# A windowed ratio with group statistics on one core: half of every second row group of batch 1 takes its denominator from channel sums made on VectorE and one wide matmul

## The chip, the cores and the metric

One of the eight cores of a Trainium2 chip runs the whole program. The metric is the device time of one execution in microseconds (us), as the median of several executions. A profile is one more execution of the same program. Engines are named as the profile names them: PE (TensorE), DVE (VectorE), ACT (ScalarE), POOL (GpSimd) and SP (SyncE, which issues the transfers).

## The reference, cut to what matters

x has the shape 2 x 128 x 128 x 192 (batch, rows, columns w, channels) in float32. It is normalised in 32 groups of 6 channels to v, and then:

```python
s     = box(v, over w, 5)
num   = box(s * s, over channels, 20)
d     = box(box(v * v, over w, 5), over channels, 20)
denum = d * c0 * c1          # c1: how many of the 5 columns lie inside, 5 but at the edges
out   = x + nan_to_num(num / denum, nan=1.0)
```

A box is a sliding sum with zeros beyond the ends. The one over channels takes 10 channels below and 9 above. In the kernel S stands for s, U for the sum of squares over w, D for the denominator (with its sign turned) and N for the numerator.

## The kernel before

Columns w lie on the 128 partitions, and rows and channels lie along each partition. A **pair** is two rows, 384 values a partition; a **duo** is two pairs, 768 values. There are 32 duos a batch and 64 in all, and the main loops of all engines run over the duos n = 0 to 63. Every PSUM tile (S, U, D, N) has two banks, one for each pair of a duo.

Both sums are matmuls with banded matrices. `box5` sums over w: the data are the stationary operand and the band b5 (or b5d, the band times -c1) moves through, so the result is transposed, channels on the partitions. It takes three matmuls of 128 columns a pair, six a duo. `box20` sums over channels: the transposed result is stationary and a band `b20` of 20 ones, already divided by the variance of each channel, moves through, which turns the result back. It takes matmuls of 138, 147 and 137 columns a pair, six a duo. The profile counts each float32 matmul as two instructions, so six matmuls stand as x12.

In batch 1 a duo passes so: POOL subtracts the group mean (`centre`, xc). PE makes S from xc with b5, and ACT squares it into a slot of xs (`square_s`). ACT squares xc (`square_xc`), PE makes U with b5d, and ACT copies U to u (`keep_u`). PE makes D from u and N from the squared S. ACT takes the reciprocal root of D (`take_root`) and squares it (`square_root`) into q. DVE makes t1 = D times q, t2 = N times q, and ratio = (t1 + 2) times t2 (`quotient`, one step of Newton's method). POOL adds the ratio to x (`finish`), and SP stores two duos at a time.

The order on each engine is fixed by the program, and semaphores connect the engines. One turn n of the main loops has

- PE: `sum_d(n)`, `box_u(n + 2)`, `sum_n(n)`, `box_s(n + 2)`. The first waits for t1 of duo n - 1, and the third for the ratio of duo n - 1.
- ACT: `take_root(n)`, `square_root(n)`, `keep_u(n + 2)`, `square_xc(n + 3)`, `square_s(n + 2)`.
- DVE: `quotient(n)`, with the late statistics of batch 1 between its steps at n = 29 (`spread_late`) and n = 30 (`scale_late_bands`).
- POOL: `centre(n + 4)`, `finish(n)`.

In batch 0 the boxes of the raw input of the first 28 duos are made ahead, while x arrives; the statistics of batch 1 are gathered on DVE during batch 0. The mean of batch 1 is known at n = 29, and POOL waits for it (semaphore mean_ready) before it centres duo 32, the first of batch 1.

`link` makes a DVE instruction whose result the next one waits for.

Of the kernel before, what the change touches and what calls it, by code (L numbers as in the profile page):

```python
# [6 lines left out]
ALU = mybir.AluOpType  # L7
# [4 lines left out]
GROUPS = 32  # L12
# [5 lines left out]
EPS = 1e-5  # L18
# [26 lines left out]

HALF = STEPS // 2
XC2_SLOT, S2_SLOT, LATE_SLOTS = HALF, HALF + 2, 2
LOADS = 8
LOAD_STEPS = STEPS // LOADS
LOAD_DUOS = LOAD_STEPS * STEP_DUOS  # L50
# [26 lines left out]
def window_ratio_kernel(nc, x, out):  # L77
    ctx = ExitStack()
    with ctx:
# [41 lines left out]
        offsets_wide_ps = S[:, 1, 0:CHUNKS * 128].rearrange("p (j w) -> p j w", j=CHUNKS)  # L121
        offsets_ps = offsets_wide_ps[:, :, 0:COEFS]

        loaded0 = [sem(f"loaded0_{j}") for j in range(LOADS)]
        loaded1 = [sem(f"loaded1_{j}") for j in range(len(LATE_SETS))]
        bands_ready = sem("bands_ready")
# [14 lines left out]
        mean_ready = sem("mean_ready")  # L141
        b20_ready = sem("b20_ready")
        inv_ready = sem("inv_ready")
        xc_ready = sem("xc_ready")
        xc2_ready = sem("xc2_ready")
        s_ready = sem("s_ready")
# [30 lines left out]
        def slot(n):  # L177

            t = n % DUOS // STEP_DUOS
            if batch(n) == 0:  # L180
                return RAW + t
            return t if t < HALF else RAW + t - HALF

        def x_rows(n, duos=1):

# [80 lines left out]
        @block.gpsimd  # L266
        def _(pool):
            own = [0]

            def band(ap, conditions):  # L270

                nc.gpsimd.memset(ap, 1.0).then_inc(pool_own, 1)
                own[0] += 1
                for base, channel, pattern in conditions:
                    pool.wait_ge(pool_own, own[0])
                    nc.gpsimd.affine_select(out=ap, in_=ap, compare_op=ALU.is_ge, fill=0.0, base=base,
                                            pattern=pattern, channel_multiplier=channel)\
# [36 lines left out]

            def finish(n):

                pool.wait_ge(ratio_ready, n + 1)
                nc.gpsimd.tensor_tensor(x_flat(n), x_flat(n), ratio[:, n % RATIO_RING, :], ALU.add)\  # L318
                  .then_inc(out_ready, 1)

            for j in range(LOADS):
                pool.wait_ge(loaded0[j], 16)
            pool.wait_ge(mean_ready, 1)
            for n in range(CENTRE_AHEAD):
                centre(n)
            for n in range(TOTAL - 1):
                m = n + CENTRE_AHEAD
                if m == DUOS:
                    for j in range(len(LATE_SETS)):
                        wait_loaded1(pool, j)  # L330
                    pool.wait_ge(mean_ready, 2)
                if m < TOTAL:
                    centre(m)
                finish(n)

        @block.scalar
        def _(act):
# [7 lines left out]
            def square_xc(n):  # L345

                act.wait_ge(xc_ready, n + 1)
                if n == RAW_DUOS:
                    act.wait_ge(n_ready, (XC2_SLOT + LATE_SLOTS) * STEP_DUOS)
                if not is_raw(n) and not is_raw(n - LATE_RING):  # L350
                    act.wait_ge(u_ready, n - LATE_RING + 1)
                nc.scalar.activation(xc2_of(n), xc_of(n), ACT.Square).then_inc(xc2_ready, 1)  # L352

            def keep_u(n):

                act.wait_ge(u_ready, n + 1)
                if n >= U_RING:
                    act.wait_ge(d_ready, n - U_RING + 1)
                nc.scalar.activation(pairs(u[:, n % U_RING, :]), in_bank(U), ACT.Copy).then_inc(us_ready, 1)  # L359

            def square_s(n):

# [57 lines left out]
            for n in range(TOTAL):  # L420
                take_root(n)
                square_root(n)
                if n + BOX_AHEAD < TOTAL:
                    keep_u(n + BOX_AHEAD)
                if n + SQUARE_AHEAD < TOTAL:
                    square_xc(n + SQUARE_AHEAD)
                square_box(n + BOX_AHEAD)

        @block.tensor
        def _(pe):  # L430

            def box5(bank, rows, weights):

                for i in range(DUO):
                    for j in range(CHUNKS):
                        chunk, at = slice(128 * j, 128 * (j + 1)), i * PCOLS + 128 * j
                        mm = nc.tensor.matmul(bank[:, i, chunk], rows[:, at:at + 128], weights[:, :],  # L437
                                              start=True, stop=True)
                return mm

            def box20(bank, data, b):

                for i in range(DUO):
# [24 lines left out]
            def box_u(n):  # L468

                pe.wait_ge(xc2_ready, n + 1)  # L470
                if n:
                    pe.wait_ge(us_ready, n)
                box5(U, xc2_of(n), b5d).then_inc(u_ready, 1)

            def sum_d(n):

                pe.wait_ge(us_ready, n + 1)
                if d_prev(n) >= 0:
                    pe.wait_ge(t1_ready, d_prev(n) + 1)
                if n == 1:  # L480
                    pe.wait_ge(edges_ready, 2)
                box20(d_bank(n), u[:, n % U_RING, :], batch(n)).then_inc(d_ready, 1)

            def sum_n(n):

# [22 lines left out]
            def average_squares(b):  # L508
# [3 lines left out]
                for j in range(CHUNKS):  # L512
                    out, cols = (var_ps[1][:, j:j + 1], 1) if b else (var_wide_ps[:, j, :], 128)
                    mm = nc.tensor.matmul(out, flat[:, 128 * j:128 * (j + 1)], averager[0][:, 0:cols],
                                          start=True, stop=True)
                return mm

            def keep_warm():
# [39 lines left out]
        def _(dve):  # L558
# [63 lines left out]
            def scale_late_bands():  # L622

                link(fold_variance(1))
                for j in range(CHUNKS):
                    cols = slice(SPAN_AT[j], SPAN_AT[j + 1])
                    ins = nc.vector.tensor_scalar(b20[:, cols], b20[:, cols], inv_var[:, j:j + 1], None, ALU.mult)
                ins.then_inc(b20_ready, 1)

            def keep_offsets():  # L630
                link(nc.vector.tensor_copy(offsets[:, :, :], offsets_ps))
# [10 lines left out]

            def quotient(n, before_ratio=None):

                dve.wait_ge(q_ready, n + 1)
                if n >= RATIO_RING:
                    dve.wait_ge(out_ready, n - RATIO_RING + 1)
# [48 lines left out]
            for n in range(TOTAL - 1):  # L696
                if n == JOIN_AT:
                    for j, g in unmeasured:
# [5 lines left out]
                quotient(n, before_ratio=spread_late if n == MEAN_AT else scale_late_bands if n == VAR_AT else None)  # L704
# [25 lines left out]
```

## Time and profile before

| what | us |
|---|---|
| median of three executions | 393.49 |
| the three executions | 393.3, 393.49, 395.51 |
| profiled execution, its own time | 395.41 |
| its span, first to last instruction | 393.6 |
| PE busy in the span | 371.3 |
| ACT, DVE, POOL busy in the span | 277.0, 262.5, 233.6 |

The span is counted in the trace from its first instruction, and every start time in the rows below is from there. The ends of matmuls are modelled, so the spacing from the start of one group to the start of the next tells more than a duration. A row `[2.48 <-ACT q L401]` says that the engine stood idle for 2.48 us before this instruction, until line 401 on ACT released it. On ACT, DVE and POOL a row's duration can overlap the start of the next instruction by up to some 0.1 us, so there too the spacing of starts is used.

### The profile page before, as it was taken

The numbers are of one execution on the slowest core, as the hardware profiler recorded it, in microseconds if no ns is written. First come the engines' busy times: TensorE is split into PE (matmuls) and PEld (weight loads), VectorE is DVE, ScalarE is ACT, GpSimd is POOL, SyncE is SP. The second block draws the span as 40 slices with busy tenths as digits, with TensorE's granted clock in tenths as the row PEclk, the third lists the DMA queues.
The fourth block names the chain that finished last, engine by engine and source line by source line (L and its number), as shares of the span: only waits on it lengthen the run. The fifth ranks groups of instructions, "written<-read, shape, count | busy, mean of one in ns | idle before, by whom it ended". The sixth has DMA issues, their size and how long they took to land.

```text
span 393.6 us, 8026 instructions
## 1 busy us (share of the span) xinstructions
PE 371.3 (94%) x3124; PEld 369.7 (94%) x3124; DVE 262.5 (67%) x555; ACT 277.0 (70%) x368; POOL 233.6 (59%) x150
## 2 busy tenths in 40 slices
PE   1999988999999999999889999999999999999982
PEld 1999988999999999999789999999999999999982
DVE  2999952676679999999766455445544455445544
ACT  1455549999999998996447667766777667766751
POOL 4000054887888888886088656765676556765431
PEclk9999989999999999999899999999999999999997
DMA  8999100588988952222203122222211222222213
GB/s 243 327 328 328 57 2 0 162 242 269 292 274 288 296 189 82 81 82 82 80 3 110 50 82 80 82 82 82 80 59 38 66 82 82 80 82 82 80 42 121
DMA packets 66485, 50.84 MB, mean 129 GB/s; under 512 B 912, under 2 KB 66448, under 8 KB 66448
## 3 DMA queue, kind: packets, MB, share of 16 engines
q1 hardware_dynamic: 66448, 50.34, 41.2%
q8 instruction: 25, 0.41, 0.4%
q14 instruction: 12, 0.10, 0.1%
HBM read 25.17 MB, written 25.17 MB: 128 GB/s over the span
## 4 chain that ended last, share of the span: by engine, by line
PE 82%; DVE 6%; issue 4%; ACT 4%; DMA 2%; POOL 0%; DVEq 0%; POOLq 0%; ACTq 0%
PE N L446 20%; PE U L437 19%; PE D L446 16%; PE S L437 16%; PE N L437 5%; PE S L446 4%; DVE late_triples L577 2%; DMA xs<-x 2%; DVE ratio L649 2%; DVE N L652 1%; ACT xs L377 1%; ACT q L395 1%; PE D L500 1%; PE U L521 1%; ACT q L401 1%
## 5 line engine op out<-in xcount | busy, mean ns | idle before, releaser
L318 POOL TENSOR_TENSOR xs<-xs,ratio 128x768 f32<-128x768 f32 x63 | 114.5, 1818 | 91.6 <-DVE ratio L658 91.6
L312 POOL TENSOR_TENSOR xc<-xs,mean_c 128x768 f32<-128x768 f32 x64 | 116.9, 1828 | 60.3 <-DVE mean_c L586 46.2
L649 DVE SCALAR_TENSOR_TENSOR ratio<-D,q 128x768 f32<-128x768 f32 x51 | 48.7, 955 | 91.7 <-ACT q L401 91.7
L652 DVE SCALAR_TENSOR_TENSOR N<-N,q 128x768 f32<-128x768 f32 x64 | 61.6, 963 | 7.5 <-PE N L446 3.9
L658 DVE SCALAR_TENSOR_TENSOR ratio<-ratio,N 128x768 f32<-128x768 f32 x64 | 61.1, 954 | 6.8 <-DVE N L652 0.5
L395 ACT ACTIVATE q<-D 128x768 f32<-128x768 f32 x51 | 41.4, 811 | 30.0 <-PE D L446 30.0
L368 ACT ACTIVATE xs<-S 128x768 f32<-128x768 f32 x36 | 29.2, 811 | 38.7 <-PE S L437 38.7
L401 ACT ACTIVATE q<-q 128x768 f32<-128x768 f32 x64 | 54.0, 844 | 2.0
L437 PE MATMUL U<-b5d,xs 128*128 128x128 f32 x432 | 54.1, 275 | 1.1 <-ACT xs L352 1.1
L437 PE MATMUL S<-b,xc 128*128 128x128 f32 x432 | 54.6, 277 | 0.0
L446 PE MATMUL N<-b_r,xs 128*128 128x138 f32 (+2 forms) x384 | 53.3, 288 | 0.0
L446 PE MATMUL D<-b,u 128*128 128x138 f32 (+2 forms) x384 | 51.6, 283 | 1.4 <-DVE ratio L649 1.4
L437 PEld LDWEIGHTS U<-b5d,xs 128*128 128x128 f32 x432 | 51.2, 191 | 1.3 <-ACT xs L352 1.3
L437 PEld LDWEIGHTS S<-b,xc 128*128 128x128 f32 x432 | 51.9, 194 | 0.0
L446 PE MATMUL N<-b,xs 128*128 128x138 f32 (+2 forms) x384 | 51.6, 283 | 0.2 <-DVE ratio L658 0.2
L359 ACT ACTIVATE u<-U 128x768 f32<-128x768 f32 x64 | 50.9, 795 | 0.3 <-PE U L437 0.2
L446 PEld LDWEIGHTS D<-b,u 128*128 128x128 f32 x384 | 48.5, 190 | 1.6 <-issue 1.6
L446 PEld LDWEIGHTS N<-b_r,xs 128*128 128x128 f32 x384 | 49.4, 193 | 0.0
L446 PEld LDWEIGHTS N<-b,xs 128*128 128x128 f32 x384 | 48.5, 190 | 0.4 <-issue 0.4
L577 DVE BATCH_NORM_STATS2 ratio<-xs 128x6 f32<-128x96 f32 x256 | 40.9, 252 | 6.0 <-DMA xs<-x 6.0
L437 PE MATMUL U<-b5d,xc 128*128 128x128 f32 x336 | 42.6, 277 | 1.2 <-ACT u L359 1.0
L437 PEld LDWEIGHTS U<-b5d,xc 128*128 128x128 f32 x336 | 40.3, 193 | 1.5 <-issue 1.2
(67 smaller groups left out, 382.2 us busy)
## 6 DMA issues: line engine op xcount, KB each, us to landing
out<-xs SPq DMA_DIRECT2D x31, 768.0 KB, 3.8
xs<-x SPq DMA_DIRECT2D x8, 1536.0 KB, 14.7
xs<-x SPq DMA_DIRECT2D x16, 768.0 KB, 5.4
out<-xs SPq DMA_DIRECT2D x2, 384.0 KB, 2.9
```

The source lines that it names most:

```text
L312: nc.gpsimd.tensor_tensor(pairs(xc[:, n % XC_RING, :]), pairs(x_flat(n)), mean, ALU.subtract)\
L318: nc.gpsimd.tensor_tensor(x_flat(n), x_flat(n), ratio[:, n % RATIO_RING, :], ALU.add)\
L359: nc.scalar.activation(pairs(u[:, n % U_RING, :]), in_bank(U), ACT.Copy).then_inc(us_ready, 1)
L368: nc.scalar.activation(pairs(s2_of(n)), in_bank(S), ACT.Square).then_inc(s2_ready, 1)
L395: nc.scalar.activation(pairs(q[:, n % Q_RING, :]), in_bank(d_bank(n)), ACT.Abs_reciprocal_sqrt, bias=-TINY)\
L401: nc.scalar.activation(q[:, n % Q_RING, :], q[:, n % Q_RING, :], ACT.Square).then_inc(q_ready, 1)
L437: mm = nc.tensor.matmul(bank[:, i, chunk], rows[:, at:at + 128], weights[:, :], start=True, stop=True)
L446: mm = nc.tensor.matmul(bank[:, i, first:end], data[:, at:at + 128], b20_r[b][:, SPAN_AT[j]:SPAN_AT[j + 1]], start=j == 0, stop=j == CHUNK ...
L577: return nc.vector.bn_stats(to.rearrange("p g a b -> p (g a b)"), rows)
L649: nc.vector.scalar_tensor_tensor(t1, in_bank(d_bank(n)), -TINY, pairs(q[:, n % Q_RING, :]), ALU.add, ALU.mult).then_inc(t1_ready, 1)
L652: nc.vector.scalar_tensor_tensor(in_bank(N), in_bank(N), TINY, pairs(q[:, n % Q_RING, :]), ALU.add, ALU.mult).then_inc(t2_ready, 1)
L658: nc.vector.scalar_tensor_tensor(t1, t1, 2.0, in_bank(N), ALU.add, ALU.mult).then_inc(ratio_ready, 1)
```

## The change

Fifteen duos of batch 1, n = 35, 37, ... 63 (`summed(n)`), treat their second pair in another way. The first pair of such a duo goes as before, so box_u, keep_u, square_xc and box20 for D work on one pair in place of two. S and N stay as they are.

For the second pair POOL multiplies xc by the reciprocal standard deviation of its channel's group (`scale_c`) into a line in SBUF, `padded`, with 10 zeros between the two rows (`normalise`). ACT squares the line of 424 values into bank 1 of U, which box_u doesn't use in this duo (`square_line`). DVE makes the sums of 20 neighbours from two scans and one addition (`sum_windows`): one scan runs backward and starts anew every 20 values, the other runs forward and starts anew at the same places, and a window of 20 is the sum of one value of each. PE then takes the result as moving operand of one matmul with b5d as stationary operand, 384 columns wide, straight into bank 1 of D.

Once, where the batches meet, the change adds what this needs: three memsets on POOL (`clear_sums`), one more small matmul for the group variance, two small steps on DVE, a reciprocal root on ACT at the end of turn 30, and on DVE in turn 31 four small steps and two copies (`spread_scale`).

```diff
+SUM_SLOT = HALF + 4
+FIRST_SUMMED, SUMMED_EVERY = DUOS + 3, 2
+PITCH = C + C_LO
+REACH = PITCH + C
+BLOCKS = (REACH + C_WIN - 1) // C_WIN
+LINE = BLOCKS * C_WIN
+PADDED = PAIR * PITCH + C_WIN
...
@@ POOL
+            def normalise(n):
+                k = nth_summed(n)
+                if k:
+                    pool.wait_ge(squares_ready, k)
+                else:
+                    pool.wait_ge(scale_ready, 1)
+                pool.wait_ge(xc_ready, n + 1)
+                pair = xc_of(n)[:, PCOLS:2 * PCOLS].rearrange("p (r c) -> p r c", r=PAIR)
+                nc.gpsimd.tensor_tensor(rows_of(padded[:, C_LO:PADDED]), pair,
+                                        scale_c.rearrange("p (r c) -> p r c", r=PAIR), ALU.mult)\
+                  .then_inc(scaled_ready, 1)
+            def clear_sums():
+                pool.wait_ge(n_ready, RAW_DUOS)
+                nc.gpsimd.memset(padded, 0.0).then_inc(pool_own, 1)
+                nc.gpsimd.memset(restart, 1.0).then_inc(pool_own, 1)
+                pool.wait_ge(pool_own, own[0] + 2)
+                nc.gpsimd.memset(restart.rearrange("p (a b) -> p a b", b=C_WIN)[:, :, 0], 0.0).then_inc(bands_ready, 1)
...
                     pool.wait_ge(mean_ready, 2)
+                    clear_sums()
                 if m < TOTAL:
                     centre(m)
+                if summed(m):
+                    normalise(m)
                 finish(n)
@@ ACT
+            def square_line(n):
+                act.wait_ge(scaled_ready, nth_summed(n) + 1)
+                act.wait_ge(us_ready, n)
+                nc.scalar.activation(squares_ps, padded, ACT.Square).then_inc(squares_ready, 1)
...
                     square_xc(n + SQUARE_AHEAD)
+                if summed(n + SQUARE_AHEAD):
+                    square_line(n + SQUARE_AHEAD)
                 square_box(n + BOX_AHEAD)
+                if n == VAR_AT:
+                    act.wait_ge(group_var_ready, 1)
+                    nc.scalar.activation(mean_sum[:, :], dev_sum[:, :], ACT.Abs_reciprocal_sqrt).then_inc(root_ready, 1)
@@ PE, box_u and sum_d
-                box5(U, xc2_of(n), b5d).then_inc(u_ready, 1)
+                if summed(n - 1):
+                    pe.wait_ge(of_20_ready, nth_summed(n - 1) + 1)
+                box5(U, xc2_of(n), b5d, own_pairs(n)).then_inc(u_ready, 1)
...
-                box20(d_bank(n), u[:, n % U_RING, :], batch(n)).then_inc(d_ready, 1)
+                mm = box20(d_bank(n), u[:, n % U_RING, :], batch(n), own_pairs(n))
+                if summed(n):
+                    pe.wait_ge(of_20_ready, nth_summed(n) + 1)
+                    mm = nc.tensor.matmul(D[:, 1, 0:PCOLS], b5d[:, :], of_20, start=True, stop=True)
+                mm.then_inc(d_ready, 1)
@@ DVE
+            def sum_windows(n):
+                k = nth_summed(n)
+                dve.wait_ge(squares_ready, k + 1)
+                if k == 0:
+                    dve.wait_ge(bands_ready, 3)
+                link(nc.vector.tensor_tensor_scan(rising[:, 0:LINE][:, ::-1], restart, squares_ps[:, 0:LINE][:, ::-1], 0.0,
+                                                  ALU.mult, ALU.add))
+                before = squares_ps[:, C_WIN - 1:C_WIN - 1 + REACH]
+                link(nc.vector.tensor_tensor_scan(before, before, restart[:, 0:REACH], 0.0, ALU.add, ALU.mult))
+                if k:
+                    dve.wait_ge(d_ready, n - SUMMED_EVERY + 1)
+                nc.vector.tensor_tensor(of_20.rearrange("p (r c) -> p r c", r=PAIR), rows_of(squares_ps[:, C_WIN - 1:PADDED]),
+                                        rows_of(rising), ALU.add).then_inc(of_20_ready, 1)
...
             def quotient(n, before_ratio=None):
+                if summed(n + 2):
+                    sum_windows(n + 2)
                 dve.wait_ge(q_ready, n + 1)
```

How the order moves on PE, in a turn n of batch 1 whose duo and whose duo n + 2 are summed (n odd). First the turn of before, from sum_d(n) to box_s(n + 2):

```order
L446 MATMUL D<-b,u 128x138
L446 MATMUL D<-b,u 128x147
L446 MATMUL D<-b,u 128x137
L446 MATMUL D<-b,u 128x138
L446 MATMUL D<-b,u 128x147
L446 MATMUL D<-b,u 128x137
L437 MATMUL U<-b5d,xs 128x128 x6
```

and the same stretch now:

```order
L520 MATMUL D<-b,u 128x138
L520 MATMUL D<-b,u 128x147
L520 MATMUL D<-b,u 128x137
L561 MATMUL D<-xs,b5d 128x384
L511 MATMUL U<-b5d,xs 128x128 x3
```

Three matmuls of D give way to a wide one, and three of U are gone; the six of N and the six of S behind them stay. In turns with even n nothing changes on PE.

On DVE the end of `quotient(n)` for even n and the start of the next one, before (t1 is L649, t2 L652, ratio L658):

```order
L649 SCALAR_TENSOR_TENSOR ratio<-D,q 128x768
L652 SCALAR_TENSOR_TENSOR N<-N,q 128x2x384
L658 SCALAR_TENSOR_TENSOR ratio<-ratio,N 128x768
L649 SCALAR_TENSOR_TENSOR ratio<-D,q 128x768
L652 SCALAR_TENSOR_TENSOR N<-N,q 128x2x384
```

and now, where the list prints a scan under the name of SCALAR_TENSOR_TENSOR (L738 and L741 are the scans, L744 the addition):

```order
L768 SCALAR_TENSOR_TENSOR ratio<-D,q 128x768
L771 SCALAR_TENSOR_TENSOR N<-N,q 128x2x384
L777 SCALAR_TENSOR_TENSOR ratio<-ratio,N 128x768
L738 SCALAR_TENSOR_TENSOR xs<-xs,U 128x400
L741 SCALAR_TENSOR_TENSOR U<-U,xs 128x394
L744 TENSOR_TENSOR xs<-U,xs 128x384
L768 SCALAR_TENSOR_TENSOR ratio<-D,q 128x768
```

The three new steps stand between the ratio of an even duo and t1 of the odd one behind it.

On POOL where the batches meet, before, with `centre(32)` as the third row:

```order
L312 TENSOR_TENSOR xc<-xs,mean_c 128x768 [waits s_ready,xc2_ready]
L318 TENSOR_TENSOR xs<-xs,ratio 128x768 [waits ratio_ready]
L312 TENSOR_TENSOR xc<-xs,mean_c 128x768 [waits xc2_ready,mean_ready,s_ready,loaded1_1,loaded1_0]
L318 TENSOR_TENSOR xs<-xs,ratio 128x768 [waits ratio_ready]
L312 TENSOR_TENSOR xc<-xs,mean_c 128x768 [waits s_ready,xc2_ready]
```

and now:

```order
L348 TENSOR_TENSOR xc<-xs,mean_c 128x768 [waits s_ready,xc2_ready]
L354 TENSOR_TENSOR xs<-xs,ratio 128x768 [waits ratio_ready]
L373 MEMSET xs 128x424 [waits mean_ready,n_ready,loaded1_1,loaded1_0]
L374 MEMSET xs 128x400
L376 MEMSET xs 128x20 [waits pool_own]
L348 TENSOR_TENSOR xc<-xs,mean_c 128x768 [waits s_ready,xc2_ready]
L354 TENSOR_TENSOR xs<-xs,ratio 128x768 [waits ratio_ready]
```

The memsets stand behind the wait for the mean and ahead of `centre(32)`.

## Rows read from the trace of the kernel before

**Rows 1.** Windows: us, busy us of PE, PEld, DVE, ACT, POOL, granted clock, DMA share, GB/s.
```profile
230.00:378.00 148.00, 148.00 (x1278) 148.00 (x1277) 76.13 (x80) 103.70 (x133) 93.07 (x52) 1.00 0.22 71
```

**Rows 2.** The chain that ended last, one turn: start us, us, what.
```profile
301.02 1.45 PE D L446 x12
302.47 1.34 PE U L437 x12
303.81 1.45 PE N L446 x12
305.25 1.34 PE S L437 x12
```

**Rows 3.** Timeline, one turn of batch 1: start us, us, engine, instruction.
```profile
300.86 1.61 PE L446 MATMUL D<-b,u 128*128 128x138 f32 x12
...
304.23 0.96 DVE L649 SCALAR_TENSOR_TENSOR ratio<-D,q 128x768 f32<-128x768 f32 x1 [2.48 <-ACT q L401]
305.29 0.97 DVE L652 SCALAR_TENSOR_TENSOR N<-N,q 128x768 f32<-128x768 f32 x1
306.36 0.95 DVE L658 SCALAR_TENSOR_TENSOR ratio<-ratio,N 128x768 f32<-128x768 f32 x1
...
302.51 0.81 ACT L395 ACTIVATE q<-D 128x768 f32<-128x768 f32 x1 [0.57 <-PE D L446]
303.35 0.84 ACT L401 ACTIVATE q<-q 128x768 f32<-128x768 f32 x1
...
301.83 1.81 POOL L318 TENSOR_TENSOR xs<-xs,ratio 128x768 f32<-128x768 f32 x1 [1.98 <-DVE ratio L658]
```

**Rows 4.** Timeline of PE around one matmul of 192 columns, in the load stage.
```profile
21.69 0.49 PE L500 MATMUL D<-ratio,averager 128*128 128x192 f32 x2
22.01 1.50 PE L437 MATMUL S<-b,xs 128*128 128x128 f32 x12
```

**Rows 5.** Timeline where the batches meet: POOL, PE, DVE, ACT.
```profile
198.47 1.82 POOL L312 TENSOR_TENSOR xc<-xs,mean_c 128x768 f32<-128x768 f32 x1 [12.11 <-issue]
...
205.57 1.82 POOL L312 TENSOR_TENSOR xc<-xs,mean_c 128x768 f32<-128x768 f32 x1
...
201.22 1.60 PE L437 MATMUL U<-b5d,xs 128*128 128x128 f32 x12 [1.14 <-ACT xs L352]
202.66 0.73 PE L514 MATMUL N<-averager,ssq_c 128*128 128x1 f32 x6
203.25 1.69 PE L446 MATMUL N<-b_r,xs 128*128 128x138 f32 x12
...
208.90 1.68 PE L446 MATMUL N<-b_r,xs 128*128 128x138 f32 x12
...
205.85 0.15 DVE L619 TENSOR_SCALAR inv_var<-N 128x3 f32<-128x3 f32 x1
...
207.81 0.94 DVE L658 SCALAR_TENSOR_TENSOR ratio<-ratio,N 128x768 f32<-128x768 f32 x1
...
207.76 0.81 ACT L395 ACTIVATE q<-D 128x768 f32<-128x768 f32 x1 [0.58 <-PE D L446]
```

**Rows 6.** Groups by line and form, POOL: mean ns of one behind the comma.
```profile
L272 POOL MEMSET b<- 128x128 f32 x1 | 0.2, 205 | 0.3 <-POOLq L723 0.3
...
L272 POOL MEMSET b<- 128x74 f32 x1 | 0.2, 162 | 0.0
```

**Rows 7.** The same view, DVE.
```profile
L627 DVE TENSOR_SCALAR b<-b,inv_var 128x138 f32<-128x138 f32 x1 | 1.2, 1232 | 0.0
...
L586 DVE COPY mean_c<-N 128x192 f32<-128x192 f32 x2 | 0.6, 347 | 0.0
...
L627 DVE TENSOR_SCALAR b<-b,inv_var 128x147 f32<-128x147 f32 x1 | 0.3, 287 | 0.0
```

**Rows 8.** Timeline of the tail: t1 of duo 62, and sum_d(63) behind it.
```profile
382.19 0.96 DVE L649 SCALAR_TENSOR_TENSOR ratio<-D,q 128x768 f32<-128x768 f32 x1 [2.48 <-ACT q L401]
...
383.29 1.68 PE L446 MATMUL D<-b,u 128*128 128x138 f32 x12 [1.41 <-DVE ratio L649]
```

More of the change, by code:

```diff
@@ L122, in window_ratio_kernel @@
         offsets_ps = offsets_wide_ps[:, :, 0:COEFS]
+        sums = xs[:, SUM_SLOT * STEP:(SUM_SLOT + 2) * STEP, :].rearrange("p r c -> p (r c)")
+        padded, restart = sums[:, 0:PADDED], sums[:, PADDED:PADDED + LINE]
+        rising, of_20 = sums[:, 1024:1024 + PADDED], sums[:, 1536:1536 + PCOLS]
+        scale_c = sums[:, 2048:2048 + PCOLS]
+        rows_of = lambda line: line[:, 0:PAIR * PITCH].rearrange("p (r c) -> p r c", r=PAIR)[:, :, 0:C]
+        squares_ps = U[:, 1, 0:PADDED]
+        group_var_ps, newton_ps = beside[1][:, 3 * GROUPS:4 * GROUPS], m2_sum[1]
         loaded0 = [sem(f"loaded0_{j}") for j in range(LOADS)]
@@ L182, in slot, with summed, nth_summed, own_pairs @@
             return t if t < HALF else RAW + t - HALF
+        def summed(n):
+            return FIRST_SUMMED <= n < TOTAL and (n - FIRST_SUMMED) % SUMMED_EVERY == 0
+        def nth_summed(n):
+            return (n - FIRST_SUMMED) // SUMMED_EVERY
+        def own_pairs(n):
+            return 1 if summed(n) else DUO
         def x_rows(n, duos=1):
@@ L351, in square_xc @@
                     act.wait_ge(u_ready, n - LATE_RING + 1)
-                nc.scalar.activation(xc2_of(n), xc_of(n), ACT.Square).then_inc(xc2_ready, 1)
+                own = own_pairs(n) * PCOLS
+                nc.scalar.activation(xc2_of(n)[:, 0:own], xc_of(n)[:, 0:own], ACT.Square).then_inc(xc2_ready, 1)
+            def square_line(n):
+                act.wait_ge(scaled_ready, nth_summed(n) + 1)
+                act.wait_ge(us_ready, n)
+                nc.scalar.activation(squares_ps, padded, ACT.Square).then_inc(squares_ready, 1)
             def keep_u(n):
@@ L358, in keep_u @@
                     act.wait_ge(d_ready, n - U_RING + 1)
-                nc.scalar.activation(pairs(u[:, n % U_RING, :]), in_bank(U), ACT.Copy).then_inc(us_ready, 1)
+                own = own_pairs(n)
+                nc.scalar.activation(pairs(u[:, n % U_RING, :])[:, 0:own, :], in_bank(U)[:, 0:own, :], ACT.Copy)\
+                  .then_inc(us_ready, 1)
             def square_s(n):
@@ L426, in _, with box5 @@
                     square_xc(n + SQUARE_AHEAD)
+                if summed(n + SQUARE_AHEAD):
+                    square_line(n + SQUARE_AHEAD)
                 square_box(n + BOX_AHEAD)
+                if n == VAR_AT:
+                    act.wait_ge(group_var_ready, 1)
+                    nc.scalar.activation(mean_sum[:, :], dev_sum[:, :], ACT.Abs_reciprocal_sqrt).then_inc(root_ready, 1)
         @block.tensor
         def _(pe):
-            def box5(bank, rows, weights):
-                for i in range(DUO):
+            def box5(bank, rows, weights, own=DUO):
+                for i in range(own):
                     for j in range(CHUNKS):
@@ L439, in box5, with box20 @@
                 return mm
-            def box20(bank, data, b):
-                for i in range(DUO):
+            def box20(bank, data, b, own=DUO):
+                for i in range(own):
                     for j, (first, end) in enumerate(SPAN):
@@ L515, in average_squares @@
                                           start=True, stop=True)
+                if b:
+                    by_group = ssq_c[:, 0, :].rearrange("p (g c) -> p g c", g=GROUPS)
+                    mm = nc.tensor.matmul(group_var_ps, averager[0][:, :], by_group[:, :, 0], start=True, stop=True)
                 return mm
@@ L628, in scale_late_bands, with fold_group_variance, spread_scale @@
                 ins.then_inc(b20_ready, 1)
+                fold_group_variance()
+            def fold_group_variance():
+                link(nc.vector.tensor_scalar(group_var_ps, group_var_ps, 1.0 / COUNT[0], EPS, ALU.mult, ALU.add))
+                nc.vector.tensor_copy(dev_sum[:, :], group_var_ps).then_inc(group_var_ready, 1)
+            def spread_scale():
+                root = mean_sum[:, :]
+                dve.wait_ge(root_ready, 1)
+                link(nc.vector.tensor_tensor(newton_ps, group_var_ps, root, ALU.mult))
+                link(nc.vector.tensor_tensor(newton_ps, newton_ps, root, ALU.mult))
+                link(nc.vector.tensor_scalar(newton_ps, newton_ps, -0.5, 1.5, ALU.mult, ALU.add))
+                link(nc.vector.tensor_tensor(root, newton_ps, root, ALU.mult))
+                for r in range(PAIR):
+                    ins = nc.vector.tensor_copy(scale_c[:, r * C:(r + 1) * C].rearrange("p (g c) -> p g c", g=GROUPS),
+                                                root.unsqueeze(2).to_broadcast([128, GROUPS, GC]))
+                ins.then_inc(scale_ready, 1)
+            def sum_windows(n):
[11 more added lines that the diff above has]
+                                        rows_of(rising), ALU.add).then_inc(of_20_ready, 1)
             def keep_offsets():
@@ L703, in _ @@
                       .then_inc(mean_sum_ready, 1)
-                quotient(n, before_ratio=spread_late if n == MEAN_AT else scale_late_bands if n == VAR_AT else None)
+                quotient(n, before_ratio=spread_late if n == MEAN_AT else scale_late_bands if n == VAR_AT else
+                         spread_scale if n == VAR_AT + 1 else None)
                 for j in range(len(LATE_SETS)):
```

6 lines of the change are left out of this document (added).

## The prediction

> **What bounds the kernel now.** I read the windows first, then the chain that ended last, then the timeline of one turn. Between 230 and 378 us PE is busy for the whole window, at a granted clock of 1.00, which is the 2.4 GHz level; ACT is busy for 103.7 of 148 us, POOL for 93.1 and DVE for 76.1 [rows 1]. The chain in this stretch holds PE alone: D 1.45, U 1.34, N 1.45, S 1.34, together 5.58 us a duo, 11.16 for two [rows 2]. The other engines follow: DVE stands idle for 2.48 us before each t1, POOL for 1.98 before each `finish` [rows 3]. So a matmul that goes away is worth its own time, for as long as the idle time of the others covers what they get in its place. The reader must check two things: how much of this cover is left, and what happens outside the steady stretch, where PE does wait: 1.14 us for the first U of batch 1 [rows 5], and in the tail [rows 8].
>
> **PE, steady stretch.** In a summed duo three of six U matmuls go: half of 1.34, 0.67 us. Three of six D matmuls go: half of 1.45, 0.725. One of 384 columns comes. No row shows 384 columns; one float32 matmul of 192 took 0.32 us from its start to the next (22.01 - 21.69) [rows 4], so twice that, 0.64. Its bounds are close: by columns at the rate of the D group (0.725 us for 422) it would be 0.66, and if it cost as much as the three that it replaces, 0.725. Net 0.67 + 0.725 - 0.64 = 0.755 us a summed duo, and with 15 of them 11.3 us (bounds 10.1 and 11.3). U and D of one pair are all that shrinks; S and N keep their 2.79 us in every duo. The new wait for of_20 in front of the wide matmul and of U of the next duo costs nothing if the windows are ready: they are made two turns ahead of D.
>
> **DVE, the loop that must stay shorter than PE's.** t1 of an odd duo now stands behind `sum_windows`, and `sum_d` of the next duo waits for t1. From there a closed loop of two turns runs, counted from the start of t1 of an odd duo: to the start of sum_d 1.10 (383.29 - 382.19 [rows 8]), to the root on ACT 1.65 (302.51 - 300.86), to the square 0.84, to t1 of the even duo 0.88, to t2 1.06, to the ratio 1.07, the ratio itself 0.95 [rows 3]: 7.55 us, and then sum_windows. PE's two turns now take 11.16 - 0.755 = 10.40. So sum_windows may take 2.85 us before PE waits for it.
>
> What it takes the trace doesn't show, since no scan stands in it. From below: at the rate of the other DVE steps. 192 values took 0.347 us [rows 7] and 768 took 0.955, the mean of those in [rows 3], so 0.145 fixed and 1.055 ns a value. Scans of 400 and 394 values are then 0.57 and 0.56, each with 0.10 of waiting for its own result (t2 to ratio is 1.07 for a step of 0.97 [rows 3]), and the addition of 384 is 0.55: 1.88 us, loop 9.43. From above: a scan needs its last sum for the next, and the slowest step a value in the rows is POOL's, 1.81 us for 768, 2.36 ns [rows 3]. With that for both scans: 0.145 + 0.94 + 0.10 = 1.19, the other 1.18, with the addition 2.92, loop 10.47, 0.07 over PE's 10.40, which is 15 x 0.07 = 1 us in all. I take no stall: the nearer rows are those of DVE, and even the far end hardly reaches PE.
>
> On this point the Trainium skill speaks against the change ("DVE: opcode table, instruction layouts, handler registers and perf-mode slots", section 6 on datapath and trigger behaviour): the built-in scan feeds its result back to an earlier stage and runs at half throughput. No run here shows it yet. An estimate by that rule, twice the 1.055 ns of the rows, gives 2.72 us for sum_windows and a loop of 10.27, which fits with 0.13 to spare.
>
> **ACT and POOL.** ACT loses half of `square_xc` and half of `keep_u` in a summed duo and gains a line of 424 values. By the row of 768 at 0.84 us [rows 3] in proportion that is -0.42, -0.42 and +0.46: nothing. Its line is ready before the ratio of that turn, behind which DVE reads it. POOL gains a multiplication of 384 values. Half of 1.81 is 0.91 us; with a strided line perhaps 1.2. It stands ahead of `finish`, in 1.98 us of idle time each turn that shrink by some 0.1. It is covered; if it took over 1.9 us, finish would be late, and even then x and xc are needed only turns later.
>
> **Where the batches meet.** This is paid once. POOL's memsets stand behind the wait for the mean and ahead of `centre(32)`, and PE's only pause there, 1.14 us, is for the square of exactly that duo [rows 5]. 128 values took 0.205 us and 74 took 0.162, so 0.8 ns a value [rows 6]: 0.44 for 424, 0.42 for 400, 0.12 for the last and some 0.05 of waiting, 1.0 us, all of it PE's. The third statistics matmul takes 0.2 (203.25 - 202.66 for three [rows 5]). On DVE two small steps come in front of ratio(30): 0.2 (like 205.85 to the next steps [rows 5]) and 0.1. Before, a scaling of 138 columns took 1.23 us where one of 147 took 0.29 [rows 7], and it ended with POOL's `centre(34)` (205.57 + 1.82 [rows 5]). Since DVE now comes 0.2 later to that place than POOL does, it loses 0.2 less there. sum_n(31), at 208.90, had followed ratio(30), ended at 208.75, without slack [rows 5]: +0.1. Together 1.0 + 0.2 + 0.1 = 1.3 us (bounds 0.9 and 2.0).
>
> The rule for this is in the Trainium skill ("SBUF — State Buffer", section "Who interferes with whom"): a DVE copy or tensor_scalar inside SBUF in a two-port mode and a GpSimd instruction exclude each other, the later one waits. The row of 1.23 us agrees with it.
>
> ACT's wait at the end of turn 30 holds the root of duo 31 (207.76 before [rows 5]): the group variance comes at about 209.1, the new root takes 0.2, so it starts at 209.35, and t1(31) ends 1.72 + 0.96 later at 212.0, ahead of sum_d(32) at 213.0 (208.90 + 1.3 + 1.45 + 1.34). Behind it t2 (to 213.15), four small steps of 0.2, two copies of 0.35, and the ratio to 215.6; sum_n(32) is due at 215.8. This fits by 0.1, no more, so it costs nothing by this count.
>
> **The sum.** 11.3 - 1.3 = 10.0 us less. Against the profiled execution this is a span of 393.6 - 10.0 = 383.6 and a time of 395.4 - 10.0 = 385.4. That execution lies 1.9 above the median, as one of the three does; against the median of 393.49 it is **383.5 us**.
>
> **Rivals.**
> - *The DVE loop becomes the bound, in part.* If scans take over 2.3 ns a value, or pay something for running backward or for writing PSUM in place, t1 of odd duos ends late, and PE waits before D of the even ones. At 3.0 ns sum_windows takes 3.42 us, 0.57 over the limit, 15 times: 8.6 us given back, 392 us. At 2.6 ns it is 3.11, 3.9 given back, 387.4. For it: the margin of 0.13 to 1.0 us in 10.4. Against: DVE is busy for barely half of the stretch [rows 1].
> - *Slower than before.* The same mechanism with a scan of which each value waits for the pipeline. From 3.52 us for sum_windows on (15 x 0.67 = 10.0), or 3.1 ns a value, all is lost. At 4.2 ns, four times the stream, it takes 4.4 us, 1.55 over: 23 us back, 407 us. For it only that no row has a scan.
> - *The wide matmul isn't cheaper than the three.* It has other rows in its way: a stationary operand of its own between those of `u`, and a wait inside the group for D. At 0.725 the saving is 0.67 a duo, 10.1 - 1.3 = 8.8 us, 384.7.
> - *The copies of the scale collide with POOL.* `spread_scale` copies inside SBUF at about 213.9, `centre(35)` runs to about 213.8. If they meet, DVE loses up to 1.8 us once and sum_n(32) has no slack: 385.2.
>
> **How the numbers follow.** PE stays the bound, with the last two rivals as its upper edge, 382.0 to 385.3: 0.66. The loop gives back a part, to 389.5: 0.17. It gives back nearly all, or something that I haven't seen does: 0.10. Slower: 0.07. A measurement of this kernel tells about 1%, or 3.9 us, from no change. So faster by over 1% (below 389.6) 0.83, within 1% 0.10, slower 0.07. The range goes from 382.0 (the memsets hidden, all else as summed) to 389.5.
>
> **What the profile after must show.** PE busy for the whole steady stretch, and the two kinds of turn: D about 1.37 and U 0.67 in the odd ones, 10.40 us for two duos. DVE idle before t1 of odd duos for 0.1 to 1.0 us, of even ones still for about 2.5. If instead PE waits there for "ratio" of the t1 line, the loop has won; the rows of the two scans tell it directly, with 1.2 us each as the limit. `centre(32)` about 1.0 us behind the end of the wait for the mean, and PE's pause for the first U of batch 1 at about 2.1 us. The prediction is wrong if the scans are slower than 2.4 ns a value, or if PE has pauses in the stretch that no wait for t1 explains.

## The result and the profile after

| kernel | median, us | executions | range |
|---|---|---|---|
| before | 394.5 | 4 | 393.3 to 395.51 |
| changed | 384.48 | 4 | 383.45 to 388.08 |

The ratio is 0.9765, 95% interval 0.9733 to 0.9796. The forecast was 383.5 in a range of 382.0 to 389.5, with ten microseconds less than before. From median to median it is 10.0 us less. The changed kernel's median itself lies 1.0 above 383.5, and so does the median of before above the 393.49 of three executions: both kernels have executions at distinct times, and a median of four falls where they happen to be mixed.

The profiled execution of the changed kernel is the slowest of its four: 388.08 us, span 386.4, mean granted clock 0.979. The others have spans of 381.7, 381.9 and 383.6. In what follows the steady stretch is read from this trace, where nothing is disturbed, and the crossing between the batches is read in several.

**The steady stretch.** The chain that ended last, two turns, as in [rows 2]:

```profile
304.60 0.73 PE D L520 x6
305.33 0.64 PE D L561 x2
305.97 0.67 PE U L511 x6
306.64 1.45 PE N L520 x12
308.09 1.34 PE S L511 x12
309.43 1.45 PE D L520 x12
...
313.66 1.34 PE S L511 x12
```

From 304.60 to the same place two turns on (315.00, where the last S ends) it is 10.40 us, where it had been 11.16. The wide matmul takes 0.64. PE alone is in the chain, and in the window, which answers to [rows 1], it is busy all the time:

```profile
225.00:372.00 147.00, 147.00 (x1220) 143.27 (x1219) 113.59 (x128) 106.14 (x155) 112.31 (x69) 1.00 0.24 76
```

DVE went from 51% busy to 77% of the stretch (113.59 of 147 us), POOL from 63% to 76%. The timeline of DVE around `sum_windows`, and of PE at the D that waits for its t1, against [rows 3]:

```profile
304.37 0.95 DVE L777 SCALAR_TENSOR_TENSOR ratio<-ratio,N 128x768 f32<-128x768 f32 x1
305.25 0.98 DVE L738 TENSOR_TENSOR_SCAN xs<-xs,U 128x400 f32<-128x400 f32 x1
306.26 0.99 DVE L741 TENSOR_TENSOR_SCAN U<-U,xs 128x394 f32<-128x394 f32 x1
307.28 0.56 DVE L744 TENSOR_TENSOR xs<-U,xs 128x384 f32<-128x384 f32 x1
307.75 0.95 DVE L768 SCALAR_TENSOR_TENSOR ratio<-D,q 128x768 f32<-128x768 f32 x1
...
312.63 0.96 DVE L768 SCALAR_TENSOR_TENSOR ratio<-D,q 128x768 f32<-128x768 f32 x1 [1.99 <-ACT q L470]
...
309.26 1.61 PE L520 MATMUL D<-b,u 128*128 128x138 f32 x12
```

The t1 of the odd duo at 307.75 follows the addition without a gap; the one of the even duo still has 1.99 us of idle time ahead of it. `sum_windows` takes 307.75 - 305.25 = 2.50 us. t1 ends at 308.70, and D starts at 309.26. Of these 0.56 us the hand-over takes 0.14 (by [rows 8]: D started 1.10 behind the start of a t1 of 0.96), so 0.42 us are free before PE would wait.

The scans and the new steps of ACT and POOL, groups by line and form (mean ns of one behind the comma):

```profile
L366 POOL TENSOR_TENSOR xs<-xc,xs 128x384 f32<-128x384 f32 x15 | 15.0, 1002 | 4.1 <-DVE xs L728 2.1
L741 DVE TENSOR_TENSOR_SCAN U<-U,xs 128x394 f32<-128x394 f32 x15 | 14.8, 986 | 0.5
L738 DVE TENSOR_TENSOR_SCAN xs<-xs,U 128x400 f32<-128x400 f32 x15 | 14.7, 981 | 0.0
...
L744 DVE TENSOR_TENSOR xs<-U,xs 128x384 f32<-128x384 f32 x15 | 8.4, 558 | 0.5
L419 ACT ACTIVATE U<-xs 128x424 f32<-128x424 f32 x15 | 7.8, 518 | 0.0
```

**The crossing.** The changed kernel's first profile, POOL and PE, against [rows 5]:

```profile
196.68 0.45 POOL L373 MEMSET xs<- 128x424 f32 x1 [11.03 <-DVE mean_c L669]
...
197.65 1.80 POOL L348 TENSOR_TENSOR xc<-xs,mean_c 128x768 f32<-128x768 f32 x1
...
193.04 0.38 PE L586 MATMUL N<-mean_sum,averager 128*128 128x32 f32 x2 [1.94 <-DVE mean_sum L821]
193.25 1.69 PE L520 MATMUL N<-b_r,xs 128*128 128x138 f32 x12
...
200.38 2.93 PE L511 MATMUL U<-b5d,xs 128*128 128x128 f32 x12 [2.65 <-ACT xs L413]
203.10 1.28 PE L594 MATMUL N<-averager,ssq_c 128*128 128x1 f32 x6
...
204.66 3.16 PE L520 MATMUL N<-b_r,xs 128*128 128x138 f32 x12
207.62 2.64 PE L511 MATMUL S<-b,xc 128*128 128x128 f32 x12
...
215.66 1.61 PE L520 MATMUL D<-b,u 128*128 128x138 f32 x12
```

The memsets take 197.65 - 196.68 = 0.97 us ahead of `centre(32)`. PE waits 2.65 us for the first U of batch 1, and behind this pause it runs at half rate: U takes 2.72 us (200.38 to 203.10) where it takes 1.34 elsewhere, N 2.96 in place of 1.45, S 2.47 in place of 1.34. The granted clock of the trace from 200.4 to 210 us is 0.50, the level of 1.2 GHz in place of 2.4. By 210.09 the rate is back. Over the whole crossing the fall costs 4.4 us, as measured next, and it is why this execution stands 4.5 us above the two fastest.

Another profile of the same kernel (run r1 below) has the same pause and no fall:

```profile
192.75 0.38 PE L586 MATMUL N<-mean_sum,averager 128*128 128x32 f32 x2 [1.93 <-DVE mean_sum L821]
...
200.09 1.60 PE L511 MATMUL U<-b5d,xs 128*128 128x128 f32 x12 [2.65 <-ACT xs L413]
...
210.96 1.61 PE L520 MATMUL D<-b,u 128*128 128x138 f32 x12
```

I measure the crossing from the matmul for the mean to D of duo 32, the first of batch 1: 215.66 - 193.04 = 22.62 us in the first trace, 210.96 - 192.75 = 18.21 in this one. From this D to the end of the span r1 has 170.7 us, and the kernel before has 181.9 in the trace of run r10, where its crossing is undisturbed too: 11.2 us less, where the prediction had 11.3 for the fifteen duos.

### The profile page after: what moved, and what is told of

Same layout as the page of the kernel before. It is cut to its first block, busy times and chain, and to the rows that moved or that the text cites. A ratio compares the mean times of both kernels' runs of the same rounds, so it can differ in the third digit from the quotient of the medians.

```text
span 386.4 us, 7863 instructions
## 1 busy us (share of the span) xinstructions
PE 362.7 (94%) x2976; PEld 356.9 (92%) x2976; DVE 296.8 (77%) x608; ACT 273.7 (71%) x384; POOL 249.7 (65%) x168
## 4 chain that ended last, share of the span: by engine, by line
PE 82%; DVE 9%; ACT 4%; DMA 2%; issue 2%; POOL 1%; DVEq 0%; POOLq 0%; ACTq 0%
PE N L520 21%; PE S L511 17%; PE U L511 17%; PE D L520 14%; PE N L511 5%; PE S L520 4%; DVE late_triples L660 3%; PE D L561 3%; DMA xs<-x 2%; DVE ratio L768 2%; DVE N L771 2%; ACT xs L446 1%; PE U L604 1%; ACT q L464 1%; DVE ratio L777 1%
## 5 line engine op out<-in xcount | busy, mean ns | idle before, releaser
L511 PEld LDWEIGHTS U<-b5d,xs 128*128 128x128 f32 x342 | 43.4, 196 | 6.6 <-ACT xs L413 2.9
L511 PE MATMUL U<-b5d,xs 128*128 128x128 f32 x342 | 45.4, 280 | 2.7 <-ACT xs L413 2.7
L427 ACT ACTIVATE u<-U 128x768 f32<-128x768 f32 x64 | 45.9, 718 | 0.8 <-PE U L511 0.7
L520 PE MATMUL D<-b,u 128*128 128x137 f32 (+2 forms) x294 | 40.8, 283 | 1.3 <-DVE ratio L768 1.3
L520 PEld LDWEIGHTS D<-b,u 128*128 128x128 f32 x294 | 37.6, 190 | 1.4 <-issue 1.4
## 6 DMA issues: line engine op xcount, KB each, us to landing
out<-xs SPq DMA_DIRECT2D x2, 384.0 KB, 2.6
```

What stands on the lines that cost most here:

```text
L427: nc.scalar.activation(pairs(u[:, n % U_RING, :])[:, 0:own, :], in_bank(U)[:, 0:own, :], ACT.Copy)\
```

## The experiments

The comparisons are to the kernel before on the same chip. Theory A: PE bounds batch 1, each summed duo gives 0.755 us, DVE's loop just fits under it, and the crossing costs 1.3 us and sometimes a fall of the clock. The rivals are those of the expectations. The executions of one kernel fall at two or three distinct times, which I call its levels and give beside the median. The kernel before has two, 393.0 to 393.8 and 395.1 to 395.5 (25 of its 57 executions). The changed kernel did not run beside r5 to r10, so its level of 383.4 comes from the first result and r1; the lowest time of before was 393.0, 393.25 and 393.21 on the three chips used, so comparisons across them are good to some 0.3 us.

**r1_changed_again.** No edit.

> The changed kernel once more, beside the next three on the same chip. Theory A (PE bounds batch 1; each summed duo gives back 0.755 us of PE time; the crossing between the batches costs 1.3 us, and some microseconds more in the executions in which TensorE's granted clock falls at the longer pause there): 10 us faster than before, 383.5 to 384.5, with a wider spread among its executions than the kernel before. Theory B (the first profile's slow crossing is the usual case): 387 to 388, 7 us faster.

Measured: 384.89 us against 393.46 before, ratio 0.9789 (0.9745 to 0.9833). With the four executions of the first result there are ten: four at 383.4 to 383.6, three at 384.8 to 385.4, three at 387.9 to 388.6, with granted clocks of 0.993 to 0.997, 0.988 and 0.979. The lowest level against the lowest of before, 383.4 to 393.2, is 9.8 us. Theory A holds, and theory B doesn't: the slow crossing is three cases in ten. The median lies 0.4 above theory A's range, for its six executions spread over three levels.

**r2_clear_early.**

```diff
-                    pool.wait_ge(mean_ready, 2)
-                    clear_sums()
+                    clear_sums()
+                    pool.wait_ge(mean_ready, 2)
```

> POOL's memsets stand ahead of the wait for the mean of batch 1, where POOL is idle anyway. Theory A: 1.0 us less than the changed kernel, since the memsets lie on the path to the first U of batch 1; centre(32) starts 0.1 us behind the mean copy, and PE's pause falls to about 1.7 us or less. Rival: the pause is set by something else (ACT, the statistics), and the time stays.

Measured: 384.02 us (382.16 to 384.12), ratio 0.9737 (0.971 to 0.9763). Its levels are 382.2 to 382.4 (two) and 384.0 to 384.1 (four); the level at 388 doesn't occur in six executions. The lower one is 1.2 below the changed kernel's lowest, where 1.0 was forecast for the memsets. The medians differ by 0.9. The timeline of PE in its profile shows the other kind of fall:

```profile
193.33 0.38 PE L586 MATMUL N<-mean_sum,averager 128*128 128x32 f32 x2 [1.93 <-DVE mean_sum L821]
193.54 2.77 PE L520 MATMUL N<-b_r,xs 128*128 128x138 f32 x12
196.10 2.12 PE L511 MATMUL S<-b,xc 128*128 128x128 f32 x12
198.06 1.61 PE L520 MATMUL D<-b_r,u 128*128 128x138 f32 x12
200.66 1.60 PE L511 MATMUL U<-b5d,xs 128*128 128x128 f32 x12 [0.99 <-ACT xs L413]
```

Here the clock fell behind the first pause, that of 1.93 us for the mean: N takes 2.56 us in place of 1.53, and S 1.96 in place of 1.34, at a granted clock of 0.52 from 194.0 to 197.5. The slow N delays the mean, which waits for it, and PE by the same 1.0 us; the slow S delays PE alone, by 0.62, and shortens the second pause to 0.99 by that. The profile of before is of this kind too, with its pause of 1.14 [rows 5]. So is the one of r4, at 395.94: its crossing takes 19.14 us, 0.9 more than in r1, and its second pause is 1.94.

**r3_clear_early_warm.** As r2, and in both pauses PE makes matmuls that nobody reads:

```diff
             def box_u(n):
+                if n == DUOS:
+                    pe.wait_ge(us_ready, n)
+                    keep_warm(times=5)
...
                 if n == MEAN_AT:
+                    keep_warm(N)
                     average_late_means()
```

> As the run before, and PE makes 8 and 5 idle matmuls into free banks where it waits at the crossing (ahead of the mean of batch 1, and ahead of the first U of batch 1). Theory A, where the pauses let the granted clock fall in some executions: no group of matmuls at half rate behind 190 us, the spread among executions falls to that of the load stage, and the median is up to 2 us below the run before. Rival, where the clock's fall is of no weight in the median: the same within 0.5 us, or slower by up to 0.5 us, because the idle matmuls end after the wait does.

Measured: 382.65 us (381.96 to 383.0), ratio 0.9711 (0.9687 to 0.9735). The spread is 1.0 us where the changed kernel had 5.2. The crossing in its trace, without half rate anywhere, takes 210.59 - 193.43 = 17.16 us, 1.05 less than in r1:

```profile
191.41 1.95 PE L608 MATMUL N<-b5d,b 128*128 128x128 f32 x16
193.43 0.41 PE L590 MATMUL N<-mean_sum,averager 128*128 128x32 f32 x2
...
199.71 1.60 PE L511 MATMUL U<-b5d,xs 128*128 128x128 f32 x12 [0.45 <-ACT xs L413]
...
210.59 1.61 PE L520 MATMUL D<-b,u 128*128 128x138 f32 x12
```

It is the fastest version of the study.

**r4_one_summed.** `FIRST_SUMMED` is `TOTAL - 1`, so one duo is summed and all of the one-off part stays.

> Only duo 63 is summed; all that the change adds where the batches meet stays. Theory A: the one-off part costs 1.3 us and one summed duo gives 0.75 back, so 0.5 us slower than the kernel before (within 1.5). Rival: the crossing costs nothing by itself, then 0.7 us faster; or it costs 3 us and more, then 2 us and more slower.

Measured: 395.03 us (393.72 to 399.22), ratio 1.004 (1.0009 to 1.007). Its lowest level, 393.7 to 394.4 (six of twelve), begins 0.6 above that of before, so the one-off part is some 1.3 us (0.6 + 0.75). Four executions lie at 395.6 to 396.0. It has the high level too, 399.1 and 399.2 in two of twelve: that belongs to the crossing and not to the summed duos.

**r5_every_third.** `SUMMED_EVERY` is 3: ten summed duos.

> Every third duo from 35 to 62 is summed, 10 in place of 15. Theory A (each summed duo is worth 0.755 us, linear, since PE alone bounds): 7.5 - 1.3 = 6.2 us faster than before, 3.8 us slower than the changed kernel. Rival (the DVE loop holds back part of the gain in every second duo): less than 2 us slower than the changed kernel.

Measured: 389.02 us (386.84 to 392.38), ratio 0.9876 (0.9833 to 0.9919), levels 386.8 to 387.1, 389.0 and 391.8 to 392.4. Lowest to lowest it is 6.4 us below before and 3.5 above the changed kernel, that is 0.70 for each of the five duos: linear, as theory A says, and not the rival's under 2. The medians alone would say 4.1, since the high level fell on four of these ten executions. Its profile is of that level, and the clock fell behind both pauses:

```profile
193.62 3.16 PE L520 MATMUL N<-b_r,xs 128*128 128x138 f32 x12
196.57 1.59 PE L511 MATMUL S<-b,xc 128*128 128x128 f32 x12
...
202.21 1.72 PE L511 MATMUL U<-b5d,xs 128*128 128x128 f32 x12 [2.61 <-ACT xs L413]
...
205.29 3.16 PE L520 MATMUL N<-b_r,xs 128*128 128x138 f32 x12
```

N alone was slow behind the first pause here, 2.95 us, and S was not, 1.42. The second pause kept its length, 2.61, so a slow N doesn't shorten it.

**r6_second_scan.** The first `link(...)` with the backward scan stands twice.

> The backward scan runs twice with the same result, so sum_windows takes 1.01 us more, 3.51 in place of 2.50. Theory A: in the changed kernel t1 of an odd duo ends 0.42 us before D of the next must start, so 0.59 us of it reach PE, 15 times: 8.9 us more than the changed kernel, PE waiting for t1 once in two turns. Rival (DVE's idle time of 2.0 us before the t1 of even duos takes it up): no change.

Measured: 394.47 us (393.32 to 398.82), ratio 1.0013 (0.9982 to 1.0045): the gain is gone. The lowest level, 393.3 to 393.5, is 9.9 above the changed kernel's, where 8.9 was expected. PE in its timeline, and t1 of an even duo:

```profile
310.49 1.69 PE L520 MATMUL D<-b,u 128*128 128x138 f32 x12 [0.44 <-DVE ratio L770]
312.01 1.50 PE L511 MATMUL U<-b5d,xs 128*128 128x128 f32 x12
...
321.57 0.60 PE L520 MATMUL D<-b,u 128*128 128x138 f32 x3 [0.45 <-DVE ratio L770]
...
313.93 0.96 DVE L770 SCALAR_TENSOR_TENSOR ratio<-D,q 128x768 f32<-128x768 f32 x1 [1.66 <-ACT q L470]
```

Two turns now take 321.57 - 310.49 = 11.08 us, 0.68 more than 10.40, which is DVE's loop: 7.55 and 3.51 for sum_windows. Of the 0.68 the expectation had 0.59; a D group that waits also takes 1.52 us to the next group (310.49 to 312.01) in place of 1.45. The wait is for t1 of the odd duo and nothing else, once in two turns, though DVE still stands idle for 1.66 us ahead of the t1 of even duos. The rival falls: idle time in the other turn can't be used.

**r7_scan_of_120.** A third scan of 120 values behind the first.

> Behind the backward scan a further one of its last 120 values, with the same result: about 0.43 us more in sum_windows, 2.93. Theory A: just the 0.42 us that are free, so no change, within 0.5 us. Rival (there is no such slack, each 0.1 us on DVE reaches PE): 6 us more.

Measured: 385.62 us (384.65 to 386.54) in four executions, ratio 0.978 (0.9744 to 0.9815). The lowest is 1.2 to 1.3 above the changed kernel's lowest, outside the 0.5 that I allowed: theory A's slack of 0.42 was taken 0.1 too large. The rival's 6 us is far off. PE:

```profile
304.15 1.50 PE L511 MATMUL S<-b,xc 128*128 128x128 f32 x12
305.51 1.68 PE L520 MATMUL D<-b,u 128*128 128x138 f32 x12
307.03 1.50 PE L511 MATMUL U<-b5d,xs 128*128 128x128 f32 x12
...
315.99 1.68 PE L520 MATMUL D<-b,u 128*128 128x138 f32 x12
```

Two turns take 10.48 us (315.99 - 305.51). D starts 1.36 behind S in place of 1.33, and U 1.52 behind D in place of 1.45: even where no idle time is listed, the D group takes 0.07 us more when t1 ends as late as this. The count of the loop, 7.55 + 2.93 = 10.48, meets it, and 0.08 us in each of 15 loops is 1.2 us.

**r8_scale_twice.** POOL's multiplication in `normalise` stands twice, the second behind the first.

> POOL multiplies each pair by its scale twice, with the same result: 1.0 us more on POOL in every second turn. Theory A: POOL isn't on the path; finish comes late by some tenths of a us, nobody waits for it: no change within 0.5 us. Rival (POOL's finish and centring are as near to the bound as DVE): over 3 us more.

Measured: 385.19 us (383.35 to 385.56) in four executions, ratio 0.976 (0.9723 to 0.9796); the levels are those of the changed kernel, 383.4 (one) and 385.2 to 385.6 (three). POOL has no part in the bound; a further 1.0 us there in every second turn is free. Its timeline shows the limit near: `finish` follows the second multiplication without idle time.

```profile
305.49 1.00 POOL L370 TENSOR_TENSOR xs<-xc,xs 128x384 f32<-128x384 f32 x1
306.45 1.82 POOL L354 TENSOR_TENSOR xs<-xs,ratio 128x768 f32<-128x768 f32 x1
```

**r9_warm_alone.** The changed kernel with idle matmuls at the two places of r3, 8 and 10 of them, and the memsets where they were.

> The changed kernel with nothing but the idle matmuls at the crossing: 8 ahead of the mean of batch 1, 10 ahead of the first U of batch 1. The changed kernel's ten executions so far lie at 383.4 to 383.6 (four), 384.8 to 385.4 (three) and 387.9 to 388.6 (three). Theory A (the two upper levels are executions in which the granted clock fell at one of the two pauses): one level is left, at 383.2 to 383.7. Rival (the levels come from elsewhere, and only the early memsets shortened the pause): three levels stay.

Measured: 383.44 us (383.3 to 383.93), ratio 0.9725 (0.9697 to 0.9752). Three of five executions are at 383.3 to 383.4 and two at 383.8 to 383.9, up to 0.2 above the expected range.

```profile
193.23 0.41 PE L590 MATMUL N<-mean_sum,averager 128*128 128x32 f32 x2
...
211.48 1.61 PE L520 MATMUL D<-b,u 128*128 128x138 f32 x12
```

The idle matmuls shorten nothing by themselves, since the crossing takes 18.25 us (211.48 - 193.23) as in r1; they take the two upper levels away. Six of the changed kernel's ten executions lay there, so five without one would be chance in about one case of a hundred; for the level at 388 alone, three of ten, five executions prove little (17%). Against r3, which also clears early, the crossing is 1.09 longer.

**r10_before_warm.** The kernel before with the same, 8 and 6.

> The kernel before with idle matmuls at the same two places, 8 and 6. Its executions lie at 393.0 to 393.9 and at 395.1 to 395.5. Theory A: the upper level goes, all executions between 392.9 and 393.6. Rival: both levels stay.

Measured: 393.54 us (393.29 to 394.32), ratio 0.9984 (0.9968 to 1.0). The level at 395.2 is gone in twelve executions, but six lie up to 0.7 above the range that I expected. The crossing of the kernel before at full rate stands in this trace:

```profile
193.51 0.41 PE L510 MATMUL N<-mean_sum,averager 128*128 128x32 f32 x2
...
210.49 1.61 PE L446 MATMUL D<-b,u 128*128 128x138 f32 x12
```

It is 16.98 us.

## Why the prediction was right

- *PE's saving a summed duo*, 0.755 us: 0.76 in the chain (11.16 to 10.40), 11.2 us for the fifteen behind the crossing, and 0.70 by r5 against the changed kernel. The 0.64 for the wide matmul, doubled from one of 192 columns, was exact; the rival in which it costs as much as the three that it replaces falls with it.
- *DVE's loop*, 7.55 us and sum_windows: r6 and r7 put it over PE's 10.40 and measured 11.08 and 10.48, both the count to 0.02. Two small errors in the 7.55 cancel there: the step behind a ratio starts 0.87 after it and not 0.95, and a D group that waits takes 0.07 more. I had summed with DVE's streaming rate and 1.88 us for sum_windows, with 2.92 as the far end, 0.07 over PE's 10.40, and took no stall. It measured 2.50.

  The scans cost 0.98 us for 400 values; with 0.145 fixed that is 2.09 ns a value, twice the 1.055 of the other steps. The 0.98 for 400 and 0.40 for 120 of r7 give 2.07 without that assumption. So the rule of the Trainium skill ("DVE: opcode table, instruction layouts, handler registers and perf-mode slots", section 6) was the better guide to the scan, and the nearest row was not; the estimate by it, 2.72, was 0.2 too high because I counted the 0.1 of waiting for its own result in full, where a scan of 0.98 is followed after 1.01, and because the steps that don't wait overlap by 0.08.

  The size of the forecast hung on the scan: the margin was 0.35 us a loop, and 0.43 us more was already paid for (r7). Its sign hung on it too, with 1 us to spare, since 1.01 more took the whole gain (r6). The sign that DVE would stand idle for 0.1 to 1.0 us before t1 of odd duos and for 2.5 before the others didn't show: t1 of an odd duo follows without idle time, and the others have 1.99. What was free lay behind t1, ahead of D.
- *ACT and POOL*: nothing, as said. In proportion to 768 values the prediction's three terms for ACT make 0.38 us less a summed duo, and they measured 0.12 less (0.51 for 0.83, 0.47 for 0.79, and 0.52 for the line), which changes nothing. POOL's multiplication took 1.00 us against the 0.91 to 1.2 of the prediction; r8 shows twice that is free.
- *The crossing*, 1.3 us: at full rate 18.21 us in r1 against 16.98 in r10, so 1.23. Of this 0.91 lies ahead of the first U of batch 1, where the memsets take 0.97 (forecast 1.0), and 0.3 behind it (forecast 0.3): the statistics matmuls take 0.81 in place of 0.59, and sum_n(31) starts 0.1 later. DVE's scaling of 138 columns took 1.01 us in r1 where it takes 1.25 in r10, the 0.2 less of the prediction. The copies of the scale, which a rival had collide with POOL, started at 211.62 in r1 as `centre(35)` ended at 211.64, and took 0.35 us together. The mechanism and the price were right.
- *The pause of PE there*, forecast at 2.1 us, was 2.65. I had added 1.0 to the 1.14 of [rows 5], and that number was from an execution in which the clock had fallen behind the pause before (N from 193.95 to 196.51 and S from there to 198.47 in the trace of before, as in r2). The slow S, 1.96 us in place of 1.34, hid 0.6 us of the pause. At full rate the changed kernel's pause is 2.65, and without the memsets' 1.0 that leaves 1.65.
- *What I missed* is the fall of the clock at this longer pause. It is 4.4 us when it happens, in three of the changed kernel's ten executions; it is shown by the traces of the first one and of r5, and by the level at 399 in r4, which has the crossing but only one summed duo. In all the versions with the longer pause and without idle matmuls (the changed kernel, r4 to r8) it came in 10 of 50 executions; in the changed kernel with idle matmuls (r3 and r9) in none of 11. It makes the changed kernel's mean worse than its median, and a median of few executions uncertain by a microsecond or more. That it never occurred in the 57 executions of before, with their shorter pause, fits. r2, with the pause shortened, hasn't shown it in six, which at one in five is no proof.

The sum was 10.0; from the traces it is 11.2 - 1.2, and lowest level to lowest level it is 9.8. That the medians of the first result differ by 10.0 as well is partly luck, since each is of four executions at two or three levels.

The two levels of the kernel before are 1.9 us apart, and the half-rate N and S explain 1.04 of it (18.02 against 16.98 for the crossing). As far as the traces show, the rest lies in the first 61 us. In every trace it takes 132.3 to 132.4 us from D of duo 0 to the matmul for the mean of batch 1, but that D starts between 60.25 (r6) and 61.31 (before). Two things differ ahead of it. Where the load stage ends, PE waits 1.13 us for the mean of batch 0, and the matmul that takes it starts between 51.33 (r1) and 52.61 (r8). Behind this pause the clock fell in ten of the twelve traces: from that matmul to D they take 8.9 to 9.0 us, at a granted clock of 0.79 from 52 to 60 us, and r6 and r8, at 1.00, take 7.66. This may also be where the range of 0.6 to 1.0 us comes from that the versions with idle matmuls keep: the execution of r9 at 383.93 reached the matmul for the mean 0.48 later than the one of r1 at 383.38.

Of the lower level of before there is no trace, so its share of this stays open. And the profile doesn't tell why the clock falls in some executions and not in others with the same pause.

## What to carry to other kernels

When a bound engine gives work to one with idle time, count the closed loop that runs through the place where the new work stands, and not the share of busy time: here DVE was 51% busy before, and 1 us on top of the 2.5 that it got in every second turn ate the whole gain (r6). Set-up that a change adds goes ahead of the wait that everybody waits behind, which was worth 1.1 us here for two exchanged lines. Where TensorE waited once for two or three microseconds, a few idle matmuls into a free bank went with the end of a loss of up to 4.4 us that a median alone hides.

## What the runs showed of the hardware

- A scan of float32 on DVE costs about 2.1 ns a value (0.98 us for 400, 0.40 for 120), running backward or forward, with its data in PSUM and the result in SBUF or in place in PSUM; an ordinary step costs 1.055.
- A float32 matmul costs the same a column at 384 columns (0.64 us) as at 192 (0.32).
- A matmul group that has to wait takes 0.07 us more: D took 1.52 us to the next group in r6, behind 0.44 us of idle time, and in r7, where none is listed; it takes 1.45 when its operands are early.
- Pauses of 1.13, 1.93 and 2.65 us on PE were each followed by a granted clock at its lower level in some executions and not in others.
- The two copies of the scale inside SBUF took less than those of the same size out of PSUM [rows 7]: a mean of 256 ns against 347 for 192 values.
